# Another order of TensorE's and ScalarE's work in the final stream's step, routing groups of 5, 5, 4 and 2 blocks, and a shorter chain for the tiles' tables

## The reference, cut to what matters

```python
h = tok_model(x)                               # final layernorm, x @ Wc.T + bc: 128 channels
xn = layernorm(h)                              # what the second model gets
y = retention(layernorm(xn)) + conv5(...)      # scan over tokens, W_out, 5-tap depthwise convolution
x1 = xn + y
x2 = x1 + gelu(layernorm(x1) @ W1.T + b1) @ W2.T + b2
h = h + x2
xf = layernorm(h)                              # input of the router
idx, sc = top_1(softmax(xf @ Wg + bg))         # one of 8 experts for each token
out = h + sc * (relu(xf @ W1[idx] + b1[idx]) @ W2[idx] + b2[idx])
```

## Time and profile before

| | us |
|---|---|
| median of three runs | 923.92 |
| the profiled execution: time | 923.91 |
| its span, first to last instruction | 921.8 |
| TensorE busy | 808.7 (88%) |
| VectorE busy | 636.4 (69%) |
| GpSimd busy | 568.9 (62%) |
| ScalarE busy | 564.4 (61%) |
| final stream begins on VectorE | 757.3 |
| last scatter issued | 859.75 |
| first tile's load issued | 863.69 |

### The profile page before, as it was taken

How to read it: one execution, slowest core, us unless ns; L and a number is a source line. 1 busy time by engine, 2 the same in 40 slices (tenths; PEclk the granted TensorE clock), 3 DMA queues, 4 the chain that set the end, 5 groups by cost and what they waited for, 6 DMA issues and landing times.

```text
span 921.8 us, 23664 instructions
## 1 busy us (share of the span) xinstructions
PE 808.7 (88%) x8467; PEld 616.3 (67%) x8467; DVE 636.4 (69%) x1961; ACT 564.4 (61%) x1558; POOL 568.9 (62%) x820
## 2 busy tenths in 40 slices
PE   4979998999999989999999899999998977886496
PEld 2767766666777656667776666777766645775396
DVE  3779966447999564579995643799956436898553
ACT  2768886347788853277888534778885313665264
POOL 3638886544488855475888554348885546668244
PEclk9989999999999989999999899999998996999599
DMA  2320000322000004230000042200000433001330
GB/s 65 105 47 3 4 14 10 115 82 81 3 4 3 17 30 135 66 100 17 4 3 17 7 131 65 81 3 4 3 3 1 131 121 150 1 14 41 92 105 24
DMA packets 38595, 43.84 MB, mean 48 GB/s; under 512 B 7162, under 2 KB 33881, under 8 KB 38345
## 3 DMA queue, kind: packets, MB, share of 16 engines
q1 hardware_dynamic: 18348, 19.40, 7.0%
q10 hardware_dynamic: 17860, 18.19, 6.3%
q0 software_dynamic: 2272, 4.74, 1.6%
HBM read 20.70 MB, written 21.59 MB: 46 GB/s over the span
## 4 chain that ended last, share of the span: by engine, by line
PE 57%; DVE 22%; issue 5%; SPq 4%; POOL 4%; ACT 4%; DMA 2%; another core or an unknown queue 0%; POOLq 0%; DVEq 0%; ACTq 0%
PE bank L1347 7%; DVE p L996 6%; DVE nmx L987 5%; PE bank L1553 5%; PE bank L1435 5%; PE bank L1554 4%; PE bank L1484 4%; PE bank L1508 4%; PE bank L1373 3%; PE bank L1384 3%; PE bank L1438 2%; PE bank L1654 2%; PE bank L1487 2%; PE bank L1663 2%; SPq L452 2%
## 5 line engine op out<-in xcount | busy, mean ns | idle before, releaser
L567 POOL TENSOR_TENSOR p<-p 128x384 f16<-128x384 f32 (+1 forms) x320 | 284.7, 910 | 101.9 <-ACT p L732 96.3
L987 DVE TENSOR_REDUCE nmx<-bank 128x1 f32<-128x384 f32 (+1 forms) x384 | 190.4, 511 | 19.4 <-PE bank L1438 15.1
L730 ACT ACTIVATE p<-bank 128x384 f32<-128x384 f32 (+1 forms) x384 | 170.9, 452 | 52.5 <-PE bank L1487 36.1
L1484 PE MATMUL bank<-stack 103*128 103x128 bf16 x1056 | 145.2, 222 | 4.5 <-DMA stack<-mtr 4.0
L732 ACT ACTIVATE p<-bank 128x384 f16<-128x384 f32 (+1 forms) x320 | 144.0, 450 | 0.0
L1487 PE MATMUL bank<-bandb,idb 128*128 128x128 bf16 x672 | 135.4, 222 | 0.0
L1508 PE MATMUL bank<-vst,p 128*128 128x49 bf16 x2112 | 116.0, 185 | 14.4 <-DVE p L996 12.8
L1435 PE MATMUL bank<-stack 100*128 100x384 bf16 (+1 forms) x384 | 121.2, 316 | 7.3 <-DVE nmx L987 2.9
L1508 PEld LDWEIGHTS bank<-vst,p 128*128 128x128 f16 x2112 | 89.6, 97 | 32.0 <-DVE p L996 18.3
L1484 PEld LDWEIGHTS bank<-stack 103*128 103x128 bf16 x1056 | 88.3, 98 | 28.5 <-issue 15.2
L1438 PE MATMUL bank<-bandb,idb 128*128 128x128 bf16 x672 | 101.2, 220 | 0.0
(11 more groups left out here) (253 smaller groups left out, 1814.9 us busy)
## 6 DMA issues: line engine op xcount, KB each, us to landing
xs<-zrow ACTq DMA_DIRECT2D x8, 2193.0 KB, 12.6
xt<-xs SPq DMA_DIRECT2D x23, 129.0 KB
w2s<-in_w SPq DMA_DIRECT2D x4, 576.0 KB
mwbs<-in_mwb SPq DMA_DIRECT2D x1, 2064.0 KB, 8.6
mw2s<-in_mw SPq DMA_DIRECT2D x1, 2048.0 KB, 12.8
lnrow<-in_lnr SPq DMA_DIRECT2D x4, 480.0 KB
stack<-mtr SPq DMA_DIRECT2D x96, 3.0 KB
w1b<-in_w SPq DMA_DIRECT2D x4, 291.0 KB
```

The costliest lines, as they stand in the source:

```text
L567: nc.gpsimd.tensor_tensor(p2[:, u % RING, 0:w], p32[:, u % RING, 0:w], p1[:, u % RING, 0:w], ALU.subtract).then_inc(p2_pool, 1)
L730: ins = nc.scalar.activation(p32[:, s % RING, 0:w], ps[2 + s % 3][:, 0:w], ACT.Exp)
L987: nc.vector.tensor_reduce(nmx[:, vn % 3, h:h + 1], nat_bank(v)[:, 0:w], AX.X, ALU.max, negate=True).then_inc(max_done, 1)
L1484: ins = mm(ps[2 + s % 3][:, blk(i)], stack[0:K_ALL, H + h, blk(m)], stack[0:K_ALL, h, blk(n)], start=True, stop=m == n)
```

## The change

Seven edits, all behind the attention layers:

1. TensorE's order in a step. Before: conv, c, m1, t0, t1, lg, m2, hw, t2, t3. After: conv, t0, c, m2, m1, t1, lg, hw, t2, t3.
2. ScalarE does a0 ahead of gelu in the step, and computes one Gelu of one element before the stream.
3. The groups have 5, 5, 4 and 2 blocks; `choose` falls in steps 17, 22, 26 and 28, `place` one step later, the last one behind the loop.
4. GpSimd's scatters begin in step 19; one in each step up to 26, two in steps 27 and 28, the others behind the loop.
5. In `place`, the slots are written ahead of the update of the counts (`seenb`), and `rank` waits for the latter alone.
6. The tables: the row of a tile comes out of fewer operations, the expert's number after it, and the count of its tokens after the first copy of weights. TensorE and VectorE wait for the experts' numbers (`experts_ready`), SyncE for the rows.
7. SyncE reads the first tile's row before it waits for the scatters. `xt` has seven buffers, not eight.

```diff
-XBUF, WBUF, OBUF = 8, 3, 4
+XBUF, WBUF, OBUF = 7, 3, 4
-BPQ = 4
-QT = NN // BPQ
+GROUPS = ((0, 5), (5, 10), (10, 14), (14, 16))
+GMAX = 5
+CHOSEN = tuple(e - 1 + DEPTH for _, e in GROUPS)
 # SyncE
             sp.wait_ge(tables, 1)
-            sp.wait_ge(scattered, 16 * NN)
             for i in range(NT):
                 row = sp.value_load(toi[0:1, 1, i:i + 1], min_val=0, max_val=ROWS - P)
+                if i == 0:
+                    sp.wait_ge(scattered, 16 * NN)
 # GpSimd, end of a step and behind the loop
-                q, k = divmod(t - (BPQ - 1) - DEPTH - 1, BPQ)
-                if 0 <= q < QT:
...
+                placed = max([0] + [e for (_, e), c in zip(GROUPS, CHOSEN) if t >= c + 2])
+                for _ in range(1 if t < NN + DEPTH - 2 else 2):
+                    if sent < placed:
+                        scatter(sent)
+                        sent += 1
+            for n in range(sent, NN):
+                scatter(n)
 # ScalarE
+            nc.scalar.activation(gs[0:1, 0, 0:1], lfa[0:1, 0:1], ACT.Gelu)
             for t in range(NN + DEPTH):
-                i = t - 9
-                if 0 <= i < NN:
-                    act.wait_ge(m1_mm, i + 1)
-                    for m in range(2):
-                        ins = nc.scalar.activation(gl[:, i % 2, m, :], ps[7][:, blk(m)], ACT.Gelu, bias=ab1s[:, m:m + 1])
-                    ins.then_inc(gelu_done, 1)
...
+                i = t - 9
+                if 0 <= i < NN:
+                    act.wait_ge(m1_mm, i + 1)
...
 # VectorE, end of place(q)
-                ch.link(nc.vector.tensor_tensor(seenb[:, :], ps[2][:, BPQ * E:(BPQ + 1) * E], seenb[:, :], ALU.add))
                 nc.vector.tensor_copy(slot[:, hb], slotf[:, hb]).then_inc(slot_ready, 1)
+                nc.vector.tensor_tensor(seenb[:, :], ps[2][:, size * E:(size + 1) * E], seenb[:, :],
+                                        ALU.add).then_inc(seen_ready, 1)
+                dve.wait_ge(seen_ready, q + 1)
 # TensorE, behind conv
+                i = t - 1
+                if 0 <= i < NN:
+                    pe.wait_ge(z0_ready, i + 1)
...
+                i = t - 6
+                if 0 <= i < NN:
                     pe.wait_ge(scan_done, i + 1)
                     mm(ps[4][:, 0:DM], st[:, i % 4, :], wos[:, :], start=False, stop=True).then_inc(c_mm, 1)
+                i = t - 10
+                if 0 <= i < NN:
+                    pe.wait_ge(gelu_done, i + 1)
...
```

More of the change, by code:

```diff
@@ L206, in program @@
         tmp = sb("tmp", [P, NT * E], F32)
+        tmp2 = sb("tmp2", [P, NT * E], F32)
+        more = sb("more", [P, E], F32)
         tof = sb("tof", [P, 5, NT], F32)
@@ L606, in _, with scatter @@
             pool.wait_ge(bo2_ready, 1)
-            for t in range(NN + DEPTH + BPQ + 1):
+            def scatter(n):
+                if n == 0:
+                    pool.wait_ge(zeroed, 16 * E)
+                g = next(g for g, (_, e) in enumerate(GROUPS) if n < e)
+                pool.wait_ge(slot_ready, g + 1)
+                nc.gpsimd.indirect_dma_start(
+                    out=xs[:, :], out_offset=bass.IndirectOffsetOnAxis(ap=slot[:, n:n + 1], axis=0),
+                    in_=trow[:, n, :], in_offset=None).then_inc(scattered, 16)
+            sent = 0
+            for t in range(NN + DEPTH):
                 i = t - 5
@@ L817, in _ @@
                                          scale=lfb[0:DHI, 0:1]).then_inc(a0_done, 1)
+                i = t - 9
+                if 0 <= i < NN:
+                    act.wait_ge(m1_mm, i + 1)
+                    for m in range(2):
+                        ins = nc.scalar.activation(gl[:, i % 2, m, :], ps[7][:, blk(m)], ACT.Gelu, bias=ab1s[:, m:m + 1])
+                    ins.then_inc(gelu_done, 1)
                 i = t - 4
@@ L836, in _ @@
                     nc.scalar.activation(xm[:, i % 2, :], ps[1][:, 0:P], ACT.Copy).then_inc(a3_done, 1)
[L837 to L838 removed]
+                if t in CHOSEN:
+                    q = CHOSEN.index(t)
                     act.wait_ge(lg_sub, q + 1)
[L840 removed]
+                    hb = slice(*GROUPS[q])
                     nc.scalar.activation(gt[:, 2, hb, :], gt[:, 1, hb, :], ACT.Exp).then_inc(lg_exp, 1)
@@ L1075, in _ @@
                             normed(i, y, zt[:, i % 4, :]).then_inc(z_ready, 1)
+            nc.vector.memset(tiles[:, 3, :], 1.0)
+            nc.vector.memset(more[:, :], 0.0)
+            nc.vector.tensor_scalar(tof[:, 2, :], tile_no, -float(P), float(P), ALU.mult, ALU.add)
             nc.vector.memset(vin[:, :, :], 1.0)
@@ L1191, in _ @@
                     normal(x1[:, i, :], h0[:, i, :], 1, 1).then_inc(x1_ready, 1)
[L1192 to L1197, removed]
+                if t in CHOSEN:
+                    choose(CHOSEN.index(t))
+                if t - 1 in CHOSEN:
+                    place(CHOSEN.index(t - 1))
+            place(len(GROUPS) - 1)
             ch.link(nc.vector.tensor_tensor(tiles[:, 4, :], seenb[:, :], base_of, ALU.subtract))
@@ L1232, in _ @@
-            ch.link(nc.vector.tensor_tensor(tof[:, 3, :], tof[:, 3, :], tof[:, 4, :], ALU.subtract))
-            ch.link(nc.vector.tensor_scalar(tof[:, 3, :], tof[:, 3, :], colc[:, 0:1], NO_TOKEN, ALU.is_le, ALU.mult))
-            ch.link(nc.vector.tensor_copy(toi[:, 2, :], tof[:, 3, :]))
-            dve.wait_ge(tables, 1)
+            ch.link(nc.vector.tensor_scalar(tof[:, 1, :], tile_no, tiles[:, 1, E - 1:E], -1.0, ALU.min, ALU.add))
+            ch.link(nc.vector.tensor_tensor(by_tile, each_tile(tof[:, 1, :]), each_e(tiles[:, 1, :]), ALU.is_ge))
@@ new lines, in _ @@
+            ch.link(nc.vector.tensor_tensor(weighted, by_tile, each_e(tiles[:, 2, :]), ALU.mult))
+            ch.link(nc.vector.tensor_reduce(tof[:, 4, :], weighted, AX.X, ALU.add))
+            ch.link(nc.vector.scalar_tensor_tensor(tof[:, 3, :], tof[:, 1, :], float(P), tof[:, 4, :], ALU.mult, ALU.add))
+            nc.vector.tensor_copy(toi[:, 1, :], tof[:, 3, :]).then_inc(tables, 1)
+            ch.link(nc.vector.tensor_reduce(tof[:, 0, :], by_tile, AX.X, ALU.add))
+            nc.vector.tensor_copy(toi[:, 0, :], tof[:, 0, :]).then_inc(experts_ready, 1)
@@ L1634, in _ @@
                     nc.tensor.transpose(ps[1][:, 0:P], trow[:, i, 0:DM], idf[:, :]).then_inc(t3_mm, 1)
-                q, k = divmod(t - (BPQ - 1) - DEPTH, BPQ)
-                if 0 <= q < QT and k == 0:
-                    rank(q)
-            pe.wait_ge(tables, 1)
+                if t in CHOSEN:
+                    rank(CHOSEN.index(t))
+            pe.wait_ge(experts_ready, 1)
             pe.wait_ge(mw_in, 48)
```

120 lines of the change are left out of this document (55 added, 65 removed).

## The result

The changed kernel took 918.52 us at the median of 20 runs (914.38 to 920.86), the kernel before 922.3 at the median of 20 runs beside them (919.04 to 926.57). The ratio is 0.9956, 95% interval 0.9945 to 0.9968: 0.44% or 4.1 us less, inside the 0.5% called "no change". In the experiments' own comparison the same changed kernel came out at 0.9973 (0.9952 to 0.9995, 12 runs): 2.5 us less. The two intervals overlap; the gain is put at 2.5 us by the one comparison and at 4.1 by the other, and no closer than that.

The account below looks back on a forecast made before the run. A TensorE-ScalarE loop of 4.12 us bounds steps to 16, GpSimd's scatters from 18 on, then SyncE waiting for the last scatter. Scatters 4.5 plus early read 0.8 make 5.3; 923.9 - 5.3 = 918.6 us, range 915 to 921.5.

Parts of the forecast that it names:

- The step's order: Stream steps on TensorE and ScalarE: step falls from 4.12 to 3.70 us, gaining 4.4 us at t0 of step 16.
- Limit (a): TensorE and ScalarE loop in a full step, t0 through gelu, a1 and the next conv: 3.70 us.
- The early Gelu: ScalarE in step 9: removes a table load of 1.28 us, nearly hidden behind m1, so worth 0.06 us.
- The step from 9 to 10 gains 0.8: Stream step without m2 in the loop: 3.26 us, a gain of 0.8 us.
- Groups and scatters: GpSimd's scatters: first at 824.9, waits of 1.73 us gone, last at 855.2 instead of 859.75, 4.5 us earlier.
- Shorter tables, seven buffers, slots ahead of counts: Tables about 1.6 us shorter, last slots 0.2 earlier, loads still some four tiles ahead: each worth 0 in the total.
- SyncE's early read: SyncE between the wait for scatters and the first tile's load: gains 0.8 us, bounds 0 and 1.0.
- The collision: Rival: VectorE and GpSimd collide, 0.3 us lost per step, 2 us in all, total 920.7; chance 0.15.
- The order did shorten the step: Answers the rival that another wait keeps the step at 4.1 us, total 923; chance 0.05.
- The slower case: Rival: t0 waits for z0, z0 behind VectorE's add waiting for c; loop 3.4 us, total 929 if slower; chance 0.05.
- An expert stage of another length: Sign of being wrong in the profile after: an expert stage whose length changed.

Follow-up runs that it names:

- the bank experiment: Changed kernel with t3's transpose result in bank 2 (back in bank 1 in the step behind each rank); ratio 0.9948 (0.9922 to 0.9975).
- m1 first: Kernel with t3 in bank 2, m1 moved straight behind t0 on TensorE, ahead of c and m2; gelu to gelu 4.10 to 4.37 us from step 10, no ratio given.
- changed kernel again: The changed kernel profiled and timed once more with no edit; ratio 0.9973 (0.9952 to 0.9995).

## Why the prediction was right, and where it wasn't

The time forecast was 918.6 and the median is 918.52, but so close a meeting is luck. The sum behind the forecast was 5.3 us, and the parts that the change explains come to 2.9. The last scatter of the same stream is at 96.44 in the mean of its six profiles (96.02 to 96.87) and at 98.42 in the one profile of before, 2.0; the way to the first load gives 3.94 - 3.07 = 0.9. The measured differences, 4.1 (2.9 to 5.1) and 2.5 (0.5 to 4.4), are in keeping with 2.9. Of the 2.4 us that the sum had too much, 1.6 are made up by its starting point: the execution of before from which it subtracts stood at 923.91, and the median of the 20 runs is 922.3. The other 0.8 is within the scatter of the runs. From 922.3 the explained 2.9 lead to 919.4, inside the range too. Of the outcomes the prediction held "faster" (by more than 0.5%) for the likeliest, at 0.62; the ratio of 0.9956 is a "same", to which it gave 0.33.

- **The step's order** was the term mis-sized. Limit (a) gave 3.70; it is 3.78 in steps 10 to 12 and 3.97 from 12 on. The order of events was right (hw free, t0 first), but t3's wait for a1, which stood in the code, was missing from (a): it puts 0.19 into each step, and the bank experiment takes it out. The other 0.08 come from conv, which has 792.63 - 791.41 = 1.22 before t0 instead of 1.11; the rest of the loop is 0.03 shorter than in (a). At t0 of step 16 the gain is 53.84 - 51.28 = 2.56 instead of 4.4: 1.07 instead of 2.3 from step 10 on, 0.70 instead of 0.8 from 9 to 10, 0.79 instead of 1.3 ahead of that.
- **The early Gelu** at 0.06 was the wrong step of the prediction. It was read against the old order, where it holds (0.04). In the new order it is worth 1.4: the order moves gelu, and the load with it, behind xa and xb, so the load starts only when m1 is done already. "The step from 9 to 10 gains 0.8" silently counted it as gone. Without it the order's gain is 1.1.
- **Groups and scatters**: choose(0) began at 817.80 after a wait of 1.48, 5.52 behind t0 of step 16 (5.2 forecast); the first scatter 14.44 behind that t0 (14.1); first to last 31.09 (30.3). Together 1.1 late, beside the 1.8 of the step. That GpSimd's waits go was right for 1.21 of the 1.73 us; the 0.52 that is left is most of what first to last took too long. But the later start takes the gain back: with groups of 4 the last scatter is where it is with 5, 5, 4 and 2.
- **Shorter tables, seven buffers, slots ahead of counts**: 0 was forecast. Only the tables were tried by a run of their own, and are worth 0; the order of slots and counts was not, and with six input buffers (the kernel with more output buffers) the ratio is that of the changed kernel. The tables have 6.2 us to spare, more than the 4 named.
- **SyncE's early read**: 0.8, right.
- **The rivals.** The collision stayed small: a normalization took 0.68 beside GpSimd's scatter instead of 0.34 (it ended at 831.72, the scatter at 831.69), and GpSimd waited 0.52 for VectorE. The order did shorten the step. The slower case didn't come here, but its loop is real, at 4.11, in the kernel with m1 first; it was priced at 3.4, and by the rows above it is 3.66: z0's end comes 2.92 behind the first add, not 2.67, because the second add comes 0.45 behind the first, where 0.20 was put. An expert stage of another length came, and was named as a sign of being wrong; it comes with either kernel.

**What stays open**: the stop of VectorE and ScalarE 37 to 38 us behind the first load, in 9 of 14 profiles. More output buffers don't take it away, and the profile doesn't show what released the two. Whether it hangs on GpSimd's drain or on something else that comes at that tile was not settled. Nor does any run tell which part of the change, if any, holds the difference between the explained 2.9 us and the measured 4.1.

## What to carry to other kernels

When an order is changed, walk the new loop through every wait in the code, also those of operations that seemed beside it: a transpose that shares a bank with the loop's output stood in line ahead of conv and cost 0.19 us in each step. A cost that is hidden in the old order has to be weighed again in the new one; the table load was worth 0.04 us in the one and 1.4 in the other. And where one execution differs from the next by 3 us, read gains between two fixed places of the trace, and look at more than one profile before explaining a stage that wasn't touched.

## What the runs showed that was not expected

- The step in which TensorE's granted clock went from 0.50 to 1.00 at the stream's start differs between executions of like streams, and moves all behind it by up to 2 us (t0 of step 7 at 20.47 instead of 18.41).
- A table load of 1.28 us had the next activation 0.01 behind its end (784.40 + 1.28, 785.69). The Trainium skill ("ScalarE: Activation LUTs", section "What ACT_TABLE_LOAD costs") has the load at 1283 ns, which agrees, and a drain of 1380 ns with it for each switch, of which these rows show nothing.
- ScalarE and VectorE stopped for 1.65 and 2.61 us (changed kernel again) and went on 0.04 us apart. TensorE's rows run on to 897.67, 0.1 us past VectorE's restart, and then it waits 1.13 us for VectorE's copy of the weights.
